# Filling products between the first images' score rows, row maxima turned by paired products, and new instruction orders

## The reference, cut to what matters

```python
# block 1 (after a group norm): attention of pixels over the first 48 channels, 16 wide
q, k, v = split(bn(einsum('oc,bchw->bohw', w_qkv, layernorm(x[:, :48]))))
attn = softmax(einsum('bcn,bcm->bnm', q, k) * scale, axis=-1)   # 1024 x 1024 for each image
out = einsum('bcn,bmn->bcm', v, attn)
x = x + bn(w_proj @ relu(concat([out, x[:, 48:]])))
# block 2 (after another group norm): attention of channels over pixels in 8 heads,
# a 3x3 depthwise convolution of the values, a channel gate with a dilated 7x7
# convolution, a spatial gate, a projection, and the second residual
```

## Time and profile before

| | |
|---|---|
| median of 3 runs | 350.49 us (349.06 to 350.73) |
| profiled execution | 349.89 us, of it span 347.8 us |
| PE busy | 313.0 us, 90% of the span |
| DVE busy | 263.1 us, 76% |
| ACT busy | 166.4 us, 48% |
| POOL busy | 23.2 us, 7% |
| mean granted clock of PE | 0.961 |

### The profile page before, as it was taken

The page is one execution under the profiler, slowest core; times in us unless marked ns, Lnnn a source line. Parts: engine busy times, 40 slices in busy tenths (PEclk is TensorE's granted clock), DMA queues, the critical chain, the costliest instruction groups (busy, mean ns, idle before and its releaser), DMA issues.

```text
span 347.8 us, 6430 instructions
## 1 busy us (share of the span) xinstructions
PE 313.0 (90%) x2680; PEld 149.6 (43%) x2680; DVE 263.1 (76%) x497; ACT 166.4 (48%) x290; POOL 23.2 (7%) x29
## 2 busy tenths in 40 slices
PE   7978998999988999998999899989998778787995
PEld 5643643342436545433553356352343354343331
DVE  7766648716599887897887598898687999748744
ACT  3242046765651579258432884156506781364320
POOL 2130100000002200002000200002000001000000
PEclk9895559999999999999999999999999999999999
DMA  8570000000000013000000430000011130013006
GB/s 227 186 199 4 0 2 0 1 2 0 3 0 2 2 32 73 2 0 2 2 1 2 123 73 2 0 2 0 2 60 33 32 73 2 2 33 73 2 0 181
DMA packets 6074, 12.45 MB, mean 36 GB/s; under 512 B 2078, under 2 KB 2718, under 8 KB 5918
## 3 DMA queue, kind: packets, MB, share of 16 engines
q1 hardware_dynamic: 5532, 11.97, 12.8%
q10 hardware_dynamic: 514, 0.08, 0.2%
HBM read 5.32 MB, written 3.15 MB: 24 GB/s over the span
## 4 chain that ended last, share of the span: by engine, by line
PE 63%; ACT 15%; DVE 14%; issue 3%; DMA 3%; SPq 1%; POOL 0%; ACTq 0%; DVEq 0%
PE psB L505 10%; ACT pT L2160 6%; DVE cx L1684 5%; PE psR L505 4%; PE psO L681 4%; PE psR L875 3%; PE psA L505 3%; PE psA L672 3%; PE psS L505 3%; DVE nmp L1544 2%; PE psO L505 2%; PE psB L990 2%; PE psA L652 2%; PE psA L875 2%; PE psB L737 1%
## 5 line engine op out<-in xcount | busy, mean ns | idle before, releaser
L1695 DVE SCALAR_TENSOR_TENSOR dd<-spp,wt,dd 112x1024 f32<-112x1024 f32 x32 | 41.1, 1283 | 4.1 <-ACT dd L2273 3.3
L1684 DVE SCALAR_TENSOR_TENSOR cx<-cpA,dw2w,cx 128x1024 f32<-128x1024 f32 x32 | 40.9, 1279 | 0.3 <-ACT cx L2192 0.2
L2160 ACT ACTIVATE pT<-psA 128x1024 f32<-128x1024 f32 x24 | 24.6, 1024 | 18.3 <-PE psA L672 18.2
L681 PE MATMUL psO<-pT,vt 128*64 128x512 f32 x96 | 25.1, 612 | 0.4
L1544 DVE TENSOR_REDUCE nmp<-psA 128x2 f32<-128x1024 f32 x16 | 19.6, 1224 | 6.4 <-PE psA L652 6.3
L1684 DVE SCALAR_TENSOR_TENSOR cx<-cpB,dw2w,cx 128x512 f32<-128x512 f32 x32 | 23.8, 743 | 0.0
L875 PE MATMUL psR<-up,wb 128*32 128x256 f32 (+1 forms) x336 | 21.1, 383 | 0.0
L1468 DVE BATCH_NORM_STATS2 st<-x 128x6 f32<-128x512 f32 x24 | 15.6, 683 | 0.7 <-DMA x<-x_dram 0.6
L672 PE MATMUL psA<-qs,ks 50*128 50x512 f32 x48 | 12.0, 496 | 3.1 <-ACT pT L2160 1.2
L2520 POOL TENSOR_TENSOR rn<-nrm,mhalf 96x4 f32<-96x4 f32 x4 | 6.5, 1633 | 115.0 <-DVE nrm L1600 115.0
L875 PEld LDWEIGHTS psR<-up,wb 128*32 128x32 f32 (+1 forms) x336 | 9.5, 109 | 9.5 <-issue 4.3
(11 more groups left out here) (452 smaller groups left out, 697.8 us busy)
## 6 DMA issues: line engine op xcount, KB each, us to landing
up<-up SPq DMA_DIRECT2D x12, 200.0 KB, 3.1
x<-x_dram SPq DMA_DIRECT2D x4, 512.0 KB, 6.3
out_dram<-x SPq DMA_DIRECT2D x8, 256.0 KB, 2.0
wt<-params_dram SPq DMA_DIRECT2D x1, 1151.5 KB, 8.5
tp<-tp SPq DMA_DIRECT2D x8, 136.0 KB, 2.4
x<-x_dram SPq DMA_DIRECT2D x8, 128.0 KB, 5.1
out_dram<-x SPq DMA_DIRECT2D x8, 128.0 KB, 2.4
wt<-params_dram SPq DMA_DIRECT2D x1, 213.5 KB, 4.3
```

The costliest lines, as they stand in the source:

```text
L681: last = mm(s.o_ps[rows(n), :], s.vt[:, t, :], s.pT[t % 2][:, n * HB:(n + 1) * HB], start=(t == 0), stop=(t == NKT - 1))
L1684: v.scalar_tensor_tensor(acc, img, dw2w[:, blk, tap:tap + 1], acc, ALU.mult, ALU.add).then_inc(cv_s.of(c), 1)
L1695: v.scalar_tensor_tensor(acc, t.spp[:, dy:dy + HH, dx:dx + WW], par("w_spdw")[:, tap:tap + 1], acc, ALU.mult, ALU.add).then_inc(dv_s.of(c), 1)
L2160: a(s.pT[t % 2][:], s.scoreT_ps[:], ACT.Exp).then_inc(ex_s.of(b), 1)
```

## The change

The lists of PE, DVE, ACT, POOL and SP are written in a new order. In PE's list there is a new call, `fill_values`, and `keep_warm` is called more often. And `max_rows` is written in another way.

```diff
             def max_rows(b):
                 s = one[SLOT1[b]]
                 pe.wait_ge(*nm_s(b, NKT + 3))
-                for t in range(NKT):
-                    last = nc.tensor.transpose(s.max_ps[0:2, t * P:(t + 1) * P], s.nmr[:, t, :].bitcast(F32), ident)
+                for t in range(4):
+                    for g in range(2):
+                        last = mm(s.max_ps[g * SP2:g * SP2 + 2, t * P:(t + 1) * P], s.nmr[:, 4 * g + t, :].bitcast(F32), ident,
+                                  start=True, stop=True)
                 last.then_inc(tm_s.of(b), 1)
...
+            def fill_values(b):
+                pe.wait_ge(*vt_s(b, 1))
+                mm(one[SLOT1[b]].o_ps[:, 0:QB], ident, wt[:, 0:QB], start=True, stop=True)
+
...
             def max_copy(b):
...
-                    a(s.qs[g * SP2:g * SP2 + 2, :], s.max_ps[0:2, g * HB:(g + 1) * HB], ACT.Copy).then_inc(qm_s.of(b), 1)
+                    a(s.qs[g * SP2:g * SP2 + 2, :], s.max_ps[g * SP2:g * SP2 + 2, 0:HB], ACT.Copy).then_inc(qm_s.of(b), 1)
...
             score_rows(0, 0)
+            fill_values(0)
             keep_warm()
             score_rows(0, 1)
+            fill_values(0)
...
             shift_t(1)
+            shift_u(1)
             store(0)
-            shift_u(1)
```

More of the change, by code:

```diff
@@ L1009, in _ @@
             keep_warm()
+            keep_warm()
+            keep_warm()
             group_means(0, 1)
@@ L1040, in _ @@
             score_rows(1, 1)
+            fill_values(1)
             scores_t(0, 1)
             pv(0, 0)
+            scores_t(0, 2)
             score_rows(1, 2)
-            scores_t(0, 2)
             score_rows(1, 3)
@@ L1047, in _ @@
             pv(0, 2)
+            scores_t(0, 3)
             score_rows(1, 4)
-            scores_t(0, 3)
             score_rows(1, 5)
@@ L1148, in _ @@
             scores_t(2, 4)
+            ci2b(0, 6)
+            scores_t(2, 5)
+            pv(2, 3)
             head_scores(1)
             norms(1)
-            scores_t(2, 5)
-            pv(2, 3)
             pv(2, 4)
-            ci2b(0, 6)
+            sp_out_a(0)
             scores_t(2, 6)
@@ L1225, in _ @@
             scores_t(3, 1)
+            attended_last(1)
+            scores_t(3, 2)
             pv(3, 0)
-            scores_t(3, 2)
-            attended_last(1)
+            k_scaled(2)
             pv(3, 1)
@@ L1743, in _ @@
             moments(0, 1)
+            setup_marks()
             setup2_a()
             setup_weights()
+            setup_bias()
             layer_norm(0)
+            setup2_b()
+            setup_slot1()
             group_stats(0, 1)
-            setup_bias()
-            setup2_b()
             q_low(0)
             k_low(0)
+            group_shift(0, 1)
             v_copy(0)
-            group_shift(0, 1)
             row_max(0, 0)
@@ L1758, in _ @@
             row_max(0, 4)
+            pixel_var(1)
             row_max(0, 5)
-            pixel_var(1)
             row_max(0, 6)
             row_max(0, 7)
-            split_max(0)
             setup2_c()
@@ L1766, in _ @@
             setup2_d()
+            split_max(0)
             q_low(1)
@@ L1786, in _ @@
             channel_stats(1, 0, 0)
+            channel_stats(0, 3, 1)
+            channel_stats(0, 3, 2)
+            block1_out(0, 1)
             channel_stats(1, 0, 1)
-            block1_out(0, 1)
             channel_stats(1, 0, 2)
@@ L1807, in _ @@
             conv2(0, 5)
+            conv2(0, 6)
+            conv2(0, 7)
             block1_out(1, 0)
             block1_out(1, 1)
+            pixel_var(2)
+            conv2(0, 8)
+            conv2(0, 9)
             channel_stats(1, 1, 0)
@@ L1812, in _ @@
             channel_stats(1, 1, 2)
[L1813 to L1817, removed]
             gram_copy(0, 0)
@@ L1858, in _ @@
             sp_conv(0, 0)
-            times_w(1)
             sp_conv(0, 1)
             sp_conv(0, 2)
+            ci1_weights(0)
+            conv2(1, 2)
             sp_conv(0, 3)
             sp_conv(0, 4)
-            conv2(1, 2)
-            conv2(1, 3)
             sp_conv(0, 5)
@@ L1885, in _ @@
             softmax_divide(1)
+            copy_uw(1)
+            conv2(1, 11)
+            conv2(1, 12)
+            attn_relu(2)
             conv2(1, 13)
             conv2(1, 14)
-            copy_uw(1)
+            gate_attended(0, 0)
             conv2(1, 15)
-            gate_one(0)
-            attn_relu(2)
-            gate_attended(0, 0)
+            copy_wmc(1)
             gate_attended(0, 1)
             gate_attended(0, 2)
-            copy_wmc(1)
             merge(0, 0)
@@ L1964, in _ @@
             merge(1, 2)
+            conv2(2, 11)
             conv2(2, 12)
-            scaled_scores(2)
             conv2(2, 13)
-            inverse_denominators(3)
             softmax_divide(2)
             result(1, 0)
+            inverse_denominators(3)
+            attn_relu(3)
             result(1, 1)
-            attn_relu(3)
-            copy_uw(2)
             conv2(2, 14)
             conv2(2, 15)
+            copy_uw(2)
+            result(1, 2)
             block1_out(3, 0)
-            result(1, 2)
+            block1_out(3, 1)
             channel_stats(1, 3, 0)
-            block1_out(3, 1)
             channel_stats(1, 3, 1)
@@ L2006, in _ @@
             conv2(3, 7)
+            conv2(3, 8)
             times_w(3)
```

253 lines of the change are left out of this document (124 added, 129 removed).

## The result

Changed 346.66 us (20 runs, 345.10 to 349.80), before 350.53 (20 runs, 347.99 to 352.99): ratio 0.9902, 95% interval 0.9876 to 0.9928, so 2.5 to 4.3 us less. Forecast were 344.0 us and 340.5 to 352.5; the gain is 3.9 us where 6.5 were forecast.

What follows compares the result with a forecast made beforehand. TensorE at half clock from 27.0 to 50.9 us, and 90% busy behind, was taken as the bound. Terms -7.2 + 0.2 + 0.3 = -6.7 took the profiled 349.89 to 343.2, said as 344.0 us; range 340.5 to 352.5.

Steps and rivals of the forecast that it cites:

- first maximum: Image 0's front, up to VectorE's first score maximum: +1.1 to +1.2 us, so at 28.0 instead of 26.87.
- first maximum to setup product: Image 0's score rows: VectorE the bound at 1.15 us a row; setup product at 36.2 against 38.08, -1.9.
- setup product to `scores_t`: Image 0, setup product to first transposed scores: at 2.4 GHz 9.06 us instead of 14.3, -7.2 in all by there.
- paired products, four images: Maxima turned by products paired on partition halves instead of transposes: 0 to +0.4 us, taken as +0.2.
- zeroings on ACT: Three zeroings between the first two exponentials, some 0.9 us in a gap of about 0.6: +0.3 us.
- orders behind: New instruction orders behind 51 us, mostly neighbours swapped: taken as 0, with 2.5 us either way.
- The sign in the clock line: If the forecast is right, no slice with 5 (half clock) stands behind 26 us in the clock line.
- the marks given as signs: Image 0: first maximum near 28.0, setup product near 36.2, first transposed scores near 45.3; later marks about 7 us early.
- Rival C: Clock falls among image 0's score rows nevertheless, so fillings cost 0.82 us each: slower, 356 us; chance 0.14.
- Rival B: Clock falls again behind the score rows, among setup products and layer norm wait: about 347 us; chance 0.18.
- The copies of `gav` ahead of the statistics: At the front, statistics work begins at 5.2 instead of 4.5 us: 0 to +0.7, taken as +0.3 us.
- Rival D: Front gains, but late block1_out(1, 0) and its statistics lose 2 us, twice that elsewhere: about 350 us; chance 0.10.

Runs made afterwards that it cites:

- e4: Changed kernel with row maxima turned by eight transposes and their copies as before, instead of paired products; 345.32 us, ratio 0.9870.
- e1: Changed kernel without the seven filling products among the score rows, the six added keep_warm kept; 353.39 us, ratio 1.0097.
- e2: Kernel before plus only the seven filling products among the score rows; six runs, median 347.50 us, the fastest three at ratio 0.9814.
- e5: Kernel before plus all 13 added fillings (seven among the rows, six keep_warm), its own orders and transposes; 346.47 us, ratio 0.9891.
- e6: Changed kernel with group matrices behind the statistics and one filling instead of three ahead of row 6; 350.24 us, ratio 1.0001.
- a2: Changed kernel with no edit, run and profiled a second time; 346.29 us, ratio 0.9895 against before.
- e7: Changed kernel's new orders alone, with none of the 13 added fillings and with transposes; 353.13 us, ratio 1.0080 against before.
- e3: Changed kernel with the copies of the group matrices behind the first image's statistics, as before; 344.41 us, ratio 0.9843.
- e9: Changed kernel, group matrices and setup_bias back in old places, without two keep_warm added between pixel_var(0) and group_means(0, 1); 343.41 us, ratio 0.9814.
- e8: Changed kernel with group matrices behind the statistics and setup_bias behind the layer norm, both as before; 344.23 us, ratio 0.9835.

## Why the prediction was right, and where it was not

| term | forecast | measured, profile |
|---|---|---|
| first maximum | +1.15 | +3.47 |
| first maximum to setup product | 8.2 for 11.21 | 9.19 |
| setup product to `scores_t` | 9.06 for 14.3 | 9.16 |
| paired products, four images | +0.2 | no difference (e4) |
| zeroings on ACT | +0.3 | 0.35 + 0.38 on the chain |
| orders behind | 0 | none left beside the zeroings |
| sum | -6.7 | -3.2 span, -3.9 median |

The sign in the clock line came true, but the marks given as signs (28.0, 36.2, 45.3) were missed by 2.3, 3.3 and 3.4 us: what follows divides that.

*Right: the clock.* From the setup product to the transposed scores the halved durations of the earlier trace rows give the measured 9.16 us to 0.1. The seven products among the rows are needed for it (e1); by themselves they were enough in three runs of six (e2), with the six `keep_warm` in all (e5). Rival C's fall among the rows came about in no profile that has the seven products; one run of e2, 355.36 us at a mean clock of 0.947, is near its 356, but was not profiled. Rival B did not come about in the change, but e6 (which also has the copies of `gav` back) shows it two products away.

*Right: the paired products cost nothing.* The rule that I set against it (the Trainium skill, "TensorE: Matmul & The Clock Gate", "Part 3: Packing small matmuls — row/col tiling") would have doubled the 1.04 us; the row of the same shape was the better guide. The Trainium skill's "Part 4: PE-mode transpose" on the same page, by which transposes don't count for the clock, made no difference here: with them it held in all six runs of e4.

*The mis-sized step: to the first maximum.* I had +1.15 and the profile has +3.47 (+1.8 in a2). It divides so, profile after against before:

- The copies of `gav` ahead of the statistics: means +1.17, where I took +0.3 of a bound of 0.7. The copies began at 5.94, not at the 5.2 of the landing row. In four other profiles with the copies there (e1, e4, e7, a2) they began at 5.08 to 5.37, and the means came at 9.39 to 9.68. The move itself costs 0.6 us (e4 against e3), twice what I took and within the bound; the rest is a late landing in this one execution.
- The five fillings behind the means: `center(0)` another +0.9 late. I took their 4.11 us as given. They took 4.63 in this profile, 3.72 in a2, whose list is the same, and 2.43 in e4, whose list is the same up to there: this is the clock, not the edit.
- Two fillings ahead of `rstd_rows(0)`: +0.93, I had +0.6. TensorE had no room there (e9 takes back 0.8; the last 0.1 is `center(0)`, whose start is still slow here).
- `setup_bias` ahead of the layer norm: +0.45 at `xn`, I had +0.3 (e8 takes it back there).
- The fillings ahead of the query and values products: `xn` to first maximum 6.34 us, 6.33 before; free, as forecast, but only because `setup_bias` makes `xn` late. With the biases in their old place it is 6.63 to 6.64 us (e5, e8, e9): I gave the fillings ahead of the query product the whole 1.5 us of the gap, and the two setup products of the biases (from 20.07 us, 0.6 us) stand in it already.

*Also too small: the score rows.* I forecast VectorE as the bound at 1.15 us a row; the gain was 2.0 us, not 3.0. The chain shows TensorE as the bound over the rows, and most of the loss over the last ones: `center(1)` 1.00, `pixel_var(1)` 0.56 and four fillings, 0.63 and 1.49, stand there one behind the other. I fitted one filling beside each row and forgot that three stand together ahead of row 6. e6 shows that they can't simply go.

*Right: nothing behind 51 us.* 295.91 us against 295.33, of which the zeroings make 0.7. Rival D (orders that lose 2 us there) is excluded by e7, whose orders lose 0.65 there. e5 says the same from the other side: fillings without any new order give the whole gain. That e7 is 2.5 us slower than before, while e5 and the change, which differ by the orders and the way the maxima are turned alone, have the same median, no run explains.

What stays open: why the clock of the first 16 us differs between executions. Runs of the changed kernel lie at 345.1 to 345.5 (seven runs, mean clock 0.992 to 0.993) and at 348.8 to 349.8 (six, 0.985), the others between; a part of the difference between any two profiles above is this spread, so the split of the front by single profiles is good to about half a microsecond or a whole one.

## What to carry to other kernels

Before a filling product is costed by its duration, look up in the clock line and in the table of stretches what clock the steps behind it have, and halve their durations if they lie in a slow stretch: here 3 us of fillings gave back 5.2 us of setup products, rows and copies. Cost orders at the front of a kernel with the landing time of each DMA in the row of the wait, and with the spread of that landing. Compare two profiles only where a product that both have takes the same time: here that turned a seeming 1.2 us into 0.6. And take fillings out one group at a time: two of them were worth some 5.5 us (e6 against e3, by their ratios), two others cost 0.8 at the mark behind them (e9).

## What the runs showed of the hardware that was not expected

- One list of instructions begins at different clocks: the same five filling products took 4.63 us in the profile of after, 3.72 in a2, the same kernel, and 2.43 in e4, whose list is the same up to there. Over all kernels with five there they took from 2.42 (e3) to 4.64 us (e5).
- The recorded clock does not always show this. In the profile of e5 it reads 1.00 while ten records take 4.64 us; in after and e4 it also reads 1.00 at the start, where 14 records of `warm_up` take 5.27 and 6.31 us, 0.38 and 0.45 each, against 0.24 for each record of `keep_warm`, of the same 256 columns, at 9.41 us in e3. The length of a known product is the better clock there.

```profile
1.77 5.27 PE L987 MATMUL psB<-xn 113*128 113x256 f32 x14 [1.77 <-POOL xn L2549]
```

```profile
1.77 6.31 PE L985 MATMUL psB<-xn 113*128 113x256 f32 x14 [1.77 <-POOL xn L2547]
```

- A slow stretch can be a full one: in e6 TensorE was busy 16.92 of 17.20 us at 1.2 GHz.
- Two products fewer decided in all 12 runs of e6, and two others in none of e9; what tells them apart no run here shows.
- The clock also fell late in two profiles, near 56 to 60 us in e1 and 267 to 271 us in e5; these two have 298 us behind `scores_t`, all others 295.3 to 297.0. In before it held there through all idle time, so one profile does not show that it will.
